# Rows of the next expert chunks gathered two chunks ahead, routing weights in their own chunk

## What is computed

```python
x = x + gnn(layernorm(x), edges, W, b)          # linear, then a sum over edges with 1/sqrt(degree) weights
h = layernorm(x)
logits = h @ router_w.T + router_b
topk_vals, topk_idx = top_k(logits, 2)          # two of eight experts for each row
topk_w = softmax(topk_vals)
for e in range(8):
    cw = sum(where(topk_idx == e, topk_w, 0))
    y = gelu(h @ w1[e].T + b1[e]) @ w2[e].T + b2[e]     # 1024 -> 512 -> 1024
    out = out + y * cw[:, None]
x = x + layernorm(out + h) * ln_w + ln_b
```

## Time and profile before

| what | value |
|---|---|
| median of 3 runs | 785.33 us (781.92 to 785.43) |
| profiled execution, its own time | 783.95 us |
| its span | 782.3 us |
| busy: PE, DVE, POOL, ACT | 609.0 us (78%), 563.1 (72%), 257.9 (33%), 230.1 (29%) |
| mean granted PE clock | 0.909 |
| chain that ended last | PE 52%; DVE 23%; DMA 10%; issue 9% |
| of it, gathers of rows (counts<-x_rows,ids) | 5% |
| DMA moved | 106.98 MB, mean 137 GB/s |

### The profile page before, as it was taken

One profiled execution on the slowest core, in us unless ns is written; L12 is line 12 of the kernel. 1 busy time (PEld: TensorE's weight loads), 2 busy tenths in 40 slices (PEclk: granted clock), 3 DMA queues, 4 the chain that ended last, 5 costly groups with the idle time before them and its releaser, 6 DMA issues.

```text
span 782.3 us, 12607 instructions
## 1 busy us (share of the span) xinstructions
PE 609.0 (78%) x3974; PEld 331.4 (42%) x3975; DVE 563.1 (72%) x1285; ACT 230.1 (29%) x317; POOL 257.9 (33%) x199
## 2 busy tenths in 40 slices
PE   1578999999999999996587499696789593959700
PEld 0234544444445454443373266354455441525300
DVE  7989999999995689999965638383747473451377
ACT  6411111111114224333442324242333332311080
POOL 6622222111220027678545504233342424030212
PEclk9999999999999999999598799898989896988955
DMA  6870000000001623433652927666675849250579
GB/s 227 315 282 1 1 0 0 0 0 0 0 1 43 262 102 135 146 128 134 189 183 88 278 107 185 222 173 233 144 264 127 279 105 324 85 84 3 109 250 258
DMA packets 35175, 106.98 MB, mean 137 GB/s; under 512 B 8961, under 2 KB 9374, under 8 KB 35102
## 3 DMA queue, kind: packets, MB, share of 16 engines
q1 hardware_dynamic: 25054, 74.38, 25.8%
q0 software_dynamic: 8896, 27.38, 15.5%
q10 hardware_dynamic: 1152, 4.19, 1.9%
HBM read 72.27 MB, written 33.67 MB: 135 GB/s over the span
## 4 chain that ended last, share of the span: by engine, by line
PE 52%; DVE 23%; DMA 10%; issue 9%; POOL 2%; DVEq 1%; ACT 1%; POOLq 1%; SPq 0%; ACTq 0%
PE ps L1398 12%; PE ps L1603 5%; DMA counts<-x_rows,ids 5%; PE ps L1604 5%; PE ps L1605 5%; PE ps L1433 4%; PE ps L1434 4%; PE ps L1435 4%; PE ps L1583 3%; PE ps L1584 3%; PE ps L1585 3%; PE ps L1565 2%; DVE last_ends L1134 2%; DMA stage<-wst_in 2%; DVE wbuf L1047 2%
## 5 line engine op out<-in xcount | busy, mean ns | idle before, releaser
L969 DVE TENSOR_SCALAR wbuf<-early,src_f 128x1250 f16<-128x1250 f16 (+1 forms) x172 | 112.2, 653 | 7.6 <-issue 7.2
L1398 PE MATMUL ps<-wbuf 128*128 128x512 f16 x516 | 103.1, 355 | 15.9 <-DVE wbuf L970 15.8
L547 POOL DMA_INDIRECT acc_rows<-work,ids_out x24 | 47.6, 1982 | 205.9 <-DVE work L1263 205.9
L432 POOL TENSOR_TENSOR work<-work 128x1024 f16<-128x1024 f32 x19 | 40.4, 2128 | 216.6 <-ACT work L678 150.6
L1583 PE MATMUL ps<-counts,wbuf 128*128 128x296 f16 (+4 forms) x256 | 76.7, 305 | 40.0 <-issue 39.2
L1221 DVE SCALAR_TENSOR_TENSOR wbuf<-stage,wbuf 128x1024 f16<-128x1024 f32 x56 | 67.1, 1218 | 14.9 <-ACT wbuf L769 14.8
L1398 PEld LDWEIGHTS ps<-wbuf 128*128 128x128 f16 x516 | 47.2, 101 | 71.7 <-DVE wbuf L970 35.1
L1584 PE MATMUL ps<-counts,wbuf 128*128 128x296 f16 (+4 forms) x256 | 76.6, 305 | 0.6 <-issue 0.6
L1603 PE MATMUL ps<-wbuf,counts 128*128 128x512 f16 x192 | 76.9, 401 | 0.0
L1604 PE MATMUL ps<-wbuf,counts 128*128 128x512 f16 x192 | 76.7, 400 | 0.0
L1585 PE MATMUL ps<-counts,wbuf 128*128 128x296 f16 (+4 forms) x256 | 76.3, 303 | 0.0
(11 more groups left out here) (270 smaller groups left out, 1102.1 us busy)
## 6 DMA issues: line engine op xcount, KB each, us to landing
stage<-wst_in SPq DMA_DIRECT2D x72, 512.0 KB, 6.5
t<-x_in SPq DMA_DIRECT2D x2, 4096.0 KB, 14.9
acc_rows<-work SPq DMA_DIRECT2D x10, 512.0 KB, 3.4
x_rows<-work SPq DMA_DIRECT2D x10, 512.0 KB, 2.6
wbuf<-b_in ACTq DMA_DIRECT2D x8, 512.0 KB, 7.3
wbuf<-acc_rows SPq DMA_DIRECT2D x8, 512.0 KB, 7.5
out_dram<-t SPq DMA_DIRECT2D x4, 512.0 KB, 11.5
out_dram<-wbuf SPq DMA_DIRECT2D x4, 512.0 KB, 7.1
```

What stands on the lines that cost most here:

```text
L969: v.tensor_scalar(onehots[:, u * OHW:u * OHW + w], iota16[:, 0:w], src_f[:, ds(k, 1)], None, ALU.is_equal)
L1398: ins = mm(count_ps[:, lo:lo + w], onehots[:, u * OHW + NP:(u + 1) * OHW], onehots[:, u * OHW + lo:u * OHW + lo + w], start=start, stop=Fa ...
```

## The change

The row buffers of even and odd chunks are now two: `gx0` (in `early`) and `gx` (in `counts`). They lie behind each other in one tensor, so that PE can take either by an address with `c % 2`. The program before the loop is as before for chunk 0 and gathers chunk 1 into `gx`. In every later step, chunk c issues the gathers of chunk c+2 between its first and second scatter-add, once chunk c+1's rows have landed. The routing weights of chunk c are no longer gathered in chunk c-1, but in chunk c with `ids_out`, after the scatter-adds of chunk c-1 have landed and `rows_added` has been given; VectorE copies them after its gelu splits and before it turns to `turned(c + 1, 0)`. POOL's loop takes two chunks per round, with one more chunk behind an `If` for an odd count; the last two chunks gather nothing. VectorE computes two more numbers for the loop's bounds.

```diff
--- before.py
+++ after.py
@@ -93,7 +93,10 @@
             return ctx.enter_context(nc.semaphore(name))
 
 
-        early = sb("early", [P, CT * D], F32)
+        rows_and_counts = sb("rows_and_counts", [P, CT * D + NT * NP * 3 // 4], F32)
+        early = rows_and_counts[:, 0:CT * D]
+        counts = rows_and_counts[:, CT * D:]
+        rows16 = rows_and_counts[:, 0:2 * CT * D].bitcast(F16)
         iota16 = early[:, 0:NP // 2].bitcast(F16)
         at = NP // 2
         zeros16 = early[:, at:at + P // 2].bitcast(F16)
@@ -104,7 +107,6 @@
         at += NP // 2
         ct_lo_8 = early[:, at:at + NP // 4].bitcast(F8)
         assert at + NP // 4 <= CT * D
-        gx0 = [early[:, i * D:(i + 1) * D] for i in range(CT)]
         ident = sb("ident", [P, P], F32)
         ident16 = sb("ident16", [P, P], F16)
         ones16 = sb("ones16", [P, P], F16)
@@ -133,7 +135,6 @@
         stage = sb("stage", [P, STAGES * D], F32)
         wbuf0 = sb("wbuf0", [P, 2 * PIECES * D], F16)
         wbuf1 = sb("wbuf1", [P, 2 * NT * D], F16)
-        counts = sb("counts", [P, NT * NP * 3 // 4], F32)
         ct_hi = counts[:, 0:NT * NP // 2].bitcast(F16)
         ct_lo = counts[:, NT * NP // 2:].bitcast(F8)
         step_from = counts[:, 0:NSTEP]
@@ -214,7 +215,7 @@
         ids_first = sb("ids_first", [P, len(FIRST)], I32)
         cw_next = sb("cw_next", [P, CT * NE], F32)
         cw_chunk = sb("cw_chunk", [P, CT * NE], F32)
-        gx = [counts[:, i * D:(i + 1) * D] for i in range(CT)]
+        gx0, gx = [[rows_and_counts[:, (b * CT + i) * D:(b * CT + i + 1) * D] for i in range(CT)] for b in range(2)]
         at = CT * D
         x4 = counts[:, at:at + DK * CH].bitcast(F16)
         at += DK * CH
@@ -489,7 +490,7 @@
 
 
             st4 = Steps(pool, pool_step4)
-            def gather_weights():
+            def gather_weights(ids):
                 for i in range(CT):
                     g.indirect_dma_start(out=cw_next[:, i * NE:(i + 1) * NE], out_offset=None, in_=cw_rows,
                                          in_offset=bass.IndirectOffsetOnAxis(ap=ids[:, i:i + 1].bitcast(U32), axis=0)
@@ -505,48 +506,53 @@
                 no = pool.value_load(chunk_at[0:1, ds(c, 1)], min_val=0, max_val=NE * CPE - 1)
                 st4.did(g.tensor_copy(into[:], slot_ids[:, ds(no * CT, CT)]))
                 st4.wait()
+                settle(pool)
 
             pool.wait_ge(x2_stored, 16 * NT + 16 * (NT - FIRST_TILES))
             pool.wait_ge(ids_in, 2 * 16)
             for i in range(len(FIRST), CT):
                 gather_first(i, ids, NT)
             pool.wait_ge(cw_stored, 16)
-            gather_weights()
+            gather_weights(ids)
             pool.wait_ge(table_loaded, 16)
             pool.wait_ge(chunks_done, 1)
             c_last = pool.value_load(last_chunk[:], min_val=NE - 1, max_val=MAXC - 3)
 
-            def chunk(c, first, last=False):
-                st4.enter(2 * c)
-                if not last:
+            def chunk(c, ahead=None, last=False):
+                if isinstance(c, int):
+                    st4.enter(0)
                     for i in range(CT):
-                        pool.wait_ge(gathered[i], 16 * c + 16)
-                    pool.wait_ge(cw_in, 16 * CT * (c + 1))
-                    settle(pool)
-                    chunk_ids(c + 1, ids)
-                    if not first:
-                        pool.wait_ge(x4_done, DK * c + DK)
-                        settle(pool)
+                        pool.wait_ge(gathered[i], 16)
+                    pool.wait_ge(cw_in, 16 * CT)
+                    chunk_ids(1, ids)
                     gather(gx)
-                    pool.wait_ge(cw_copied, c + 1)
-                    settle(pool)
-                    gather_weights()
-                if first:
                     add_lnb(NT - 2)
                     add_lnb(NT - 1)
+                    chunk_ids(0, ids_out)
                 else:
+                    st4.enter(2 * c if last else 2 * c + 1)
                     for i in range(CT):
                         pool.wait_ge(added[i], 16 * c)
                     pool.sem_inc(rows_added, 1)
-                if last:
-                    pool.sem_inc(last_adds, 1)
-                chunk_ids(c, ids_out)
+                    if last:
+                        pool.sem_inc(last_adds, 1)
+                    chunk_ids(c, ids_out)
+                    pool.wait_ge(cw_copied, c)
+                    settle(pool)
+                    gather_weights(ids_out)
                 for i in range(CT):
                     pool.wait_ge(y_ready, CT * c + (i + 1))
                     settle(pool)
                     g.indirect_dma_start(out=acc_rows, out_offset=bass.IndirectOffsetOnAxis(
                         ap=ids_out[:, i:i + 1].bitcast(U32), axis=0), in_=y_out[i], in_offset=None,
                         compute_op=ALU.add).then_inc(added[i], 16)
+                    if ahead is not None and i == 0:
+                        for k in range(CT):
+                            pool.wait_ge(gathered[k], 16 * c + 32)
+                        pool.wait_ge(x4_done, DK * c + DK)
+                        settle(pool)
+                        chunk_ids(c + 2, ids)
+                        gather(ahead)
                     if last and i:
                         pool.wait_ge(added[i - 1], 16 * c + 16)
                         pool.sem_inc(last_adds, 1)
@@ -554,10 +560,16 @@
                     pool.wait_ge(added[CT - 1], 16 * c + 16)
                     pool.sem_inc(last_adds, 1)
 
-            chunk(0, True)
-            with pool.Fori(1, c_last) as c:
-                chunk(c, False)
-            chunk(c_last, False, True)
+            last_1 = pool.value_load(over_i[0:1, 1:2], min_val=NE - 2, max_val=MAXC - 4)
+            last_2 = pool.value_load(over_i[0:1, 2:3], min_val=NE - 3, max_val=MAXC - 5)
+            chunk(0, gx0)
+            with pool.Fori(0, last_2 // 2) as pair:
+                chunk(pair * 2 + 1, gx)
+                chunk(pair * 2 + 2, gx0)
+            with pool.If(last_2 % 2):
+                chunk(last_2, gx)
+            chunk(last_1)
+            chunk(c_last, last=True)
 
 
             g.iota(out_no, [[P, NT]], base=0, channel_multiplier=1).then_inc(out_no_done, 1)
@@ -1183,7 +1195,9 @@
             st3.link(v.tensor_tensor(scan[:, 0, 0:NE], scan[:, 3, NE:], ranges2_f[:, 0, :], ALU.subtract))
             st3.link(v.tensor_copy(ranges2_f[:, 0, :], scan[:, 0, 0:NE]))
             v.tensor_copy(ranges2[:], ranges2_f[:]).then_inc(ranges2_done, 1)
-            st3.link(v.tensor_scalar(last_chunk[:], ranges2_f[:, 1, NE - 1:NE], -1.0, None, ALU.add))
+            for k, ap in enumerate((last_chunk[:], over_i[0:1, 1:2], over_i[0:1, 2:3])):
+                st3.did(v.tensor_scalar(ap, ranges2_f[:, 1, NE - 1:NE], -(k + 1.0), None, ALU.add))
+            st3.wait()
             first_turned(2)
 
             over_e = [1, MAXC, NE]
@@ -1246,6 +1260,8 @@
                     dve.wait_ge(gelu_done, c * FK + (FK + f + 1))
                     st4.link(v.tensor_copy(y_hi[:, fs], y32[:, fs]))
                     v.tensor_tensor(y_lo[:, fs], y32[:, fs], y_hi[:, fs], ALU.subtract).then_inc(y_lo_done, 1)
+                if not first:
+                    weights_of(c)
                 dve.wait_ge(cw_copied, c + 1)
                 dve.wait_ge(rows_added, c + 1)
                 if not last:
@@ -1271,7 +1287,6 @@
                     return
                 dve.wait_ge(y_ready, c * CT + CT)
                 v.tensor_copy(hold[:, 1:2], hold[:, 0:1]).then_inc(y_ready_b2, 1)
-                weights_of(c + 1)
 
             LINKS4 = FK
 
@@ -1562,8 +1577,9 @@
                     if j == 0:
                         pe.wait_ge(gathered[i], c * 16 + 16)
                     for h in range(2):
-                        ins = mm(x4_ps[j % 2][:, i * P:(i + 1) * P], gx[i].bitcast(F16)[:, h * D + j * P:h * D + (j + 1) * P],
-                                 ident16[:], start=(h == 0), stop=(h == 1), skip_group_check=True)
+                        at = c % 2 * (2 * CT * D) + ((2 * i + h) * D + j * P)
+                        ins = mm(x4_ps[j % 2][:, i * P:(i + 1) * P], rows16[:, ds(at, P)], ident16[:],
+                                 start=(h == 0), stop=(h == 1), skip_group_check=True)
                 ins.then_inc(x4_done, 1)
 
             def up(c, w_hi, w_lo, wide=CH, first=0):
```

## The result

The changed kernel takes 789.93 us (median of nine runs), the kernel before 782.55 in the same measurement. The ratio is 1.0105 [1.0073, 1.0138]: the change makes the kernel **slower by 1%**. One of the nine, 1620.85 us, was disturbed; the ratio leaves it out, and the other eight lie between 788.63 and 795.02. I had forecast 779 and gave "slower" 0.24; 789.93 lies inside the range of 769 to 792.

A forecast was written before the change was run, and what follows sets the result against it. PE, busy 78% of the span, was taken as the bound, waiting for gathered rows in chunks 2, 3 and 5. 783.95 - 5.4 (gain there) + 0.6 (register addresses, VectorE operations) = 779.2, taken as 779; range 769 to 792.

The forecast's parts named there:

- y+20.4: Landing of a chunk's routing weights, counted from y, when the previous chunk's last output piece is scaled; bounds y+17.6 and y+25.8.
- y+12.0: Landing of a chunk's third scatter-add after y (last output piece scaled), with gathers queued ahead; bounds 10.5 and 15.1.
- 4.9 + 3.5: From the scatter-adds' landing: 4.9 us to issue ids copy and three small weight gathers, 3.5 until the third lands.
- The share of DMA in `down`: DMA engines' busy share during a chunk's second product, claimed to rise from 0.40 to about 0.6.
- The step that failed in sign: PE's issue gaps between chunks were counted as unchanged; otherwise the forecast would be wrong altogether, should they change with traffic.
- the register addresses: PE's transposes taking their address from a register: 0.3 us charged, bound 6 us; chance 0.04 of not being hidden.
- The gain of 5.4 us: k1, second matmul group of `down`, earlier in chunks 2, 3 and 5: gains of 1.4, 1.6 and 2.4 us.
- the forecast's 23.2: Start of k1 (second group of `down`) after y, last output scaled: y+21.6 plus 1.6 for the clock.
- the 1.6 us for the clock: Charge for PE's lower clock in k1, second group of `down`, after idling 2 to 4 us before it.
- proof of early weights: Sign: PE not idle after k0, first group of `down`; rival claims up to 14.9 us gain, chance 0.22.
- the new wait is just as long as the old one: Rival: weights at y+22, k1 at y+24.8; gains 0 to 1 us, time 783 to 787; chance 0.20.
- slower by the weights chain: Rival: gathers delay later scatter-adds; chunks lose from weights at y+22.0 to 22.8 on, up to 14 us, 798; chance 0.24.

The follow-up runs named there:

- e2_regs: The kernel before, with only its transposes' addresses taken from a register: 792.46 us, 1.0157 of the kernel before.
- h2_both_widths2: `g2_early_widths2` with the transposes' buffer address a constant: 720.71 us, 0.9268 of the kernel before.
- e7_after_pad128: The changed kernel with 128 idle semaphore instructions early in PE's program: 780.22 us, 0.9958 of the kernel before.
- g4_before_widths2: The kernel before, with two versions of a chunk's width in PE's code instead of four: 754.87 us, 0.9641 of the kernel before.
- h1_after_widths2: The complete changed kernel with two versions of a chunk's width instead of four: 762.65 us, 0.9804 of the kernel before.
- g2_early_widths2: The changed kernel with routing weights gathered a chunk ahead, as before the change, and two width versions instead of four: 723.17 us, 0.9243 of the kernel before.

## Why the prediction was wrong

**What held.** The row gather is awaited by PE nowhere after chunk 0, and a new wait stands before VectorE's copy of the weights, in chunks 2, 3 and 5, 22.2 us in all. The copies come at 505.4, 546.3 and 635.4, which is y+21.8, y+21.4 and y+21.3; I had y+20.4 with bounds of 17.6 and 25.8. The second scatter-add of chunk 2 leaves at 521.7 where I had 521.9, but that is luck: the chunk runs 1.3 us late, and from the first scatter-add it is 7.8 us and not 9.3. The gathers took 0.9 to 1.4 us each in that stretch, not 1.9. The third lands 13.6 to 14.2 us after its issue (tile `acc_rows`, chunks 1 to 3), where it had taken 9.7:

```profile
DMA to landing us min/median/max: 13.6/13.6/13.6
...
DMA to landing us min/median/max: 14.2/14.2/14.2
```

That is y+14.4 at the least, and not the y+12.0 that I took between 10.5 and 15.1. The argument for the low end (the queue now runs in a quiet stretch) was wrong by 2.4 us; what follows was in turn about 1.2 us quicker than my 4.9 + 3.5. The share of DMA in `down` is 0.36 and 0.39 (504.4 to 522.6 and 544.0 to 561.8 us), not 0.6.

**The step that failed in sign** is the last sentence of the prediction's working: the issue gaps were counted as unchanged. They were 8.1 us of the loss in chunk 4 (5.1 and 3.0), which no term of the sum held. The forecast's last sentence names the danger but looks for it in the traffic; `e2_regs`, with the traffic of before, shows it in PE's code. I priced the register addresses at 0.3 us, bounded by 6, as work of the engine; as such they cost nothing that can be measured (`h2_both_widths2`; 723.17 and 720.71 us, on two chips). The row used for it, L1433, was a fair one for that. What it could not show is the size and position of the code: 528 instructions more, 11 us by `e2_regs` (792.46 against 781.61), and 10 us back by 128 idle ones (`e7_after_pad128`).

**The gain of 5.4 us** in chunks 2, 3 and 5 failed at the same step: it came out as 1.0 (1.3 and 0.7 won in 3 and 5, 1.0 lost in 2). The forecast lets k0 start right behind the old gap, at y+16.1, 13.9 and 16.2, and hides it behind the weights. With gaps of 7.75, 3.85 and 6.83 us k0 came at y+20.7, 17.6 and 19.7 and k1 at 25.5, 23.3 and 24.7, against the forecast's 23.2, which has the clock loss in it. The weights, 1 to 1.4 us later than forecast, held PE up only in chunk 3, by 0.6 us. That k1 came as forecast there is luck: the later weights and the 1.6 us for the clock, which was not lost behind so short a wait, cancel. That also spoils one of my signs: PE is not idle after k0 in chunks 2 and 5, which I had called proof of early weights; k0 itself was late.

**A second error shows only without the gaps.** The forecast takes today's k1, 24.6 to 25.6 us after y, as what the weights must beat, but part of that lag is the gap: the earlier trace rows shows "issue" with 4.08 us in front of the first transpose of chunk 2 and 4.24 in chunk 5. In `g4_before_widths2`, where PE waits for nothing but rows in the loop, k1 comes 22.7 to 24.3 after y. In `h1_after_widths2` the weights let k1 begin at 22.2 to 23.4, where I had 21.6, and it then runs at the lower clock, as I had charged; k2 is later in all four chunks. What I had as the rival "the new wait is just as long as the old one" (0.20) is what the change does by its own mechanism, and a little more: 0.9804 against 0.9641.

The rival "slower by the weights chain" put the slower side down to weights at y+22.0 and later. (For chunk 2 my own sum gives 24.6 - 2.8 = 21.8; 22.0 is chunk 3's.) They were at y+21.8, 21.4 and 21.3 in chunks 2, 3 and 5, short of its threshold or just at it. In the program with gaps its sign was right by another cause; in the program without them (y+20.5 to 21.4 by the copies of chunks 2 to 5) the threshold itself was too late by 1 us or more, since it was taken from the same lag with the gap in it: with weights at y+20.5 chunks 4 and 5 lost already. The bounds from the rows, 10.5 to 15.1 and 17.6 to 25.8, held all that was measured of those two steps.

**What stays open.** Which of the jumps finds its code loaded was read from PE's records and not derived from the addresses, so I can't say at which size of the loop between two and three versions the gaps begin, nor why 64 idle instructions leave the time alone and 128 don't. That 128 help is shown for two kernels at one position each. Gaps of 4.8 to 6.7 us in front of `up` in chunks 1 and 7, outside the loop, remain with two versions too. Why the weights of chunk 6 come at y+23.2 in `h1_after_widths2` stays unexplained.

## What to carry to other kernels

Before a wait is moved, subtract from the lag everything that isn't that wait, "issue" gaps above all, and ask what is next: here the rows and the weights were due within 2 us of each other, and only the kernel that waits for neither was fast (723.2 us against 754.9). An "issue" gap of some microseconds in front of the first instruction behind a branch was code being fetched here; look for packets in the instruction queue, and try less code in the loop even if the engine then computes more. A comparison of two kernels with such gaps has a noise of its own, some 10 us here, which repeated runs don't show; move the code by idle instructions, or remove the gaps, before a few tenths of a per cent are put down to a cause.

## What the runs showed of the hardware beyond that

- Instruction packets of 16 KB on queue q8, whose number changes with PE's program: from 470 to 700 us 25 in the changed kernel, and 13 in `g2_early_widths2`. On the pages, 54 and 34 for the whole run:

```profile
q8 instruction: 54, 0.88, 0.4%
...
q8 instruction: 34, 0.56, 0.3%
```

- The 0.9 MB that such packets move are nothing beside 107 MB; what costs is the stop of the sequencer, 3 to 6.6 us at a time, with the DMA engines at 327 GB/s in the gap of chunk 4 (563 to 574 us).
- With an address in a register, 12 transposes in a row take 1.80 us (592.24, above) instead of 0.84, 0.15 us each. In the kernels without gaps in the loop this costs nothing that the time shows (`h2_both_widths2`).
- The clock was at its lower level behind a wait of 5.99 us (0.52 for 4.6 us, above) and also behind one of 2.29, at a cost of 1.6 to 2 us each, so a wait removed is worth more than its length: from `g4_before_widths2` to `g2_early_widths2` 22.4 us of waits go, the busy time of PE falls from 614.6 to 602.8 us for the same 3974 matmuls, and the time by 31.7 us.
